# Scatter of an edge-attention layer as four rounded-type passes, with the edge rows split on GpSimd and new per-engine lists

## The reference

```python
e = jnp.einsum('behd,hd->beh', leaky_relu(Qs + Kt, 0.2), a) + jnp.log(A0[src, dst] + EPS)[None, :, None]
attn = ex / denom[src]                       # softmax over the edges of one source node
Y = jax.ops.segment_sum(attn[..., None] * Vt, src, num_segments=n)
return Y.reshape(bt, n, d) @ W_out.T
```

## Time and profile before

| what | value |
|---|---|
| median of 3 runs | 1133.86 us (1133.8 to 1134.31) |
| the profiled execution's own time | 1133.88 us |
| its span, first to last instruction | 1132.0 us |
| mean granted TensorE clock, share of full speed | 0.989 |
| instructions | 21408 |

### The profile page before, as it was taken

The page is one execution under the profiler, slowest core; times in us unless marked ns, Lnnn a source line. Parts: engine busy times, 40 slices in busy tenths (PEclk is TensorE's granted clock), DMA queues, the critical chain, the costliest instruction groups (busy, mean ns, idle before and its releaser), DMA issues. The chain is left out here.

```text
span 1132.0 us, 21408 instructions
## 1 busy us (share of the span) xinstructions
PE 1083.0 (96%) x7105; PEld 866.6 (77%) x7105; DVE 853.7 (75%) x3073; ACT 757.9 (67%) x1640; POOL 344.9 (30%) x465
## 2 busy tenths in 40 slices
...
DMA packets 132941, 89.42 MB, mean 79 GB/s; under 512 B 13664, under 2 KB 115424, under 8 KB 132832
## 3 DMA queue, kind: packets, MB, share of 16 engines
...
...
## 5 line engine op out<-in xcount | busy, mean ns | idle before, releaser
L2360 ACT ACTIVATE att_Es<-att_Ts,att_small 128x512 f32<-128x512 f32 x256 | 184.9, 724 | 8.9 <-DVE att_small L2457 8.2
L2457 DVE CUSTOM_DVE_ANT_0 att_Ts<-bank,mask_att 128x512 f32<-128x512 f32 x256 | 172.0, 683 | 22.4 <-PE bank L2612 18.3
L2369 ACT COPY att_PTs<-bank 128x512 f32<-128x512 f32 x248 | 144.5, 583 | 51.9 <-PE bank L2665 51.1
L2665 PE MATMUL bank<-ident,att_Es 128*128 128x128 f32 x1024 | 155.8, 275 | 6.8 <-ACT att_PTs L2369 6.6
L2665 PEld LDWEIGHTS bank<-ident,att_Es 128*128 128x128 f32 x1024 | 121.3, 142 | 42.8 <-ACT att_PTs L2369 17.3
L2612 PE MATMUL bank<-K_parts,Q_parts 128*128 128x512 f32 x256 | 113.1, 471 | 5.5 <-DVE att_small L2457 3.9
L2154 POOL TENSOR_SCALAR n_rs<-n_mv 128x4 f32<-128x4 f32 x46 | 15.5, 338 | 282.4 <-DVE n_mv L2149 282.4
L1597 PE MATMUL bank<-G_hi,UT_parts 128*128 128x384 f32 x288 | 79.1, 345 | 1.8 <-DVE G_lo L1440 1.8
L567 PE MATMUL bank<-gat_whs,gat_ETs 128*128 128x128 f32 x512 | 63.7, 280 | 2.0 <-PEq L149 2.0
L784 POOL TENSOR_SCALAR l_rs<-l_mv 128x4 f32<-128x4 f32 x16 | 3.8, 236 | 198.6 <-DVE l_mv L1064 198.2
L2612 PEld LDWEIGHTS bank<-K_parts,Q_parts 128*128 128x128 f32 x256 | 45.5, 190 | 24.2 <-issue 13.5
...
## 6 DMA issues: line engine op xcount, KB each, us to landing
Q_parts<-q_hi SPq DMA_DIRECT2D x128, 64.0 KB, 2.2
Q_parts<-q_lo SPq DMA_DIRECT2D x128, 64.0 KB, 2.0
K_parts<-k_hi SPq DMA_DIRECT2D x128, 64.0 KB, 2.0
K_parts<-k_lo SPq DMA_DIRECT2D x128, 64.0 KB, 2.0
...
```

The source lines that it names most:

```text
L2360: nc.scalar.activation(att_E[:, j % RING_E, :], att_T[:, j % RING_T, :], ACT.Exp, scale=-1.0, bias=att_small[:, 0, j:j + 1], accum_out=att ...
L2369: nc.scalar.copy(att_PT[:, h, :, cols(q)], c2[:].rearrange("p (s q) -> p s q", q=P)).then_inc(sem("att_pt"), 1)
L2457: nc.vector.tensor_tensor_reduce(att_T[:, j % RING_T, :], [c0, c1][j % 2][:], k.mask_att[:, tile_of(n, j)[1], :], -QK_SCALE, HUGE, ALU.add ...
L2665: mm = nc.tensor.transpose(dst[:, cols(s)], att_E[:, i % RING_E, cols(s)], k.ident[:])
```

## The change

edge_scatter now multiplies two parts of U, U_hi and U_lo, each in the type float32r, by src_rows, which is stored as float32r too: four matmuls where two stood. A new GpSimd step, edge_parts, makes the parts once edge_u is done: U_hi is a copy of U into float32r, U_lo is U - U_hi. edge_scatter waits for edge_parts (edge_ulo) instead of edge_u. The parts lie in the memory of edge_hgs, which is free between edge_v and edge_yT. The scratch gb gets a name of its own, fc_rows, at the same place as src_rows. In the front edge_parts(0) is the last GpSimd step. FILL_ORDER, ORDER and DRAIN_ORDER are new for all engines; every step and batch that was there is there again, and edge_parts is added to GpSimd's lists. The diff, without FILL_ORDER and DRAIN_ORDER:

```diff
--- before.py
+++ after.py
@@ -50,7 +50,7 @@
     edge_x edge_lcol edge_xz edge_le edge_exp edge_scattered edge_yT gat_done edge_stat edge_z edge_lb edge_max
     edge_lc edge_den edge_rden edge_attn edge_v edge_u x3_stored cheb_h edge_done ffn_y3 gat_turned gat_zloaded
     gat_loaded gat_aggr gat_vareps gat_rs gat_small gat_exp gat_s2 gat_hT gat_wh gat_pv gat_whs gat_max
-    gat_eturn gat_eT gat_stat gat_normed gat_T gat_rinv
+    edge_uhi edge_ulo gat_eturn gat_eT gat_stat gat_normed gat_T gat_rinv
 """.split()
 
 
@@ -103,7 +103,9 @@
         with ExitStack() as front:
             zsplit = sb("z_split", [P, 2, 2, N], R32, front)
         edge_pick = sb("edge_pick", [P, NT, 2 * E], R32)
-        src_rows = sb("src_rows", [P, ET, N])
+        with ExitStack() as front:
+            fc_rows = sb("fc_rows", [P, ET * N], F32, front)
+        src_rows = sb("src_rows", [P, ET, N], R32)
         seg_bias = sb("seg_bias", [P, ET, E])
         same_src = sb("same_src", [P, ET, E])
         logA = sb("logA", [P, ET])
@@ -133,7 +135,7 @@
                    x1_dram=x1_dram, x3_dram=x3_dram, res_dram=res_dram, v_dram=v_dram, rowv=rowv, b1c=b1c,
                    ident=ident, ones=ones, neg_half=neg_half, lap_hi=lap_hi, lap_lo=lap_lo, mask_gat=mask_gat,
                    mask_att=mask_att, zsplit=zsplit, edge_pick=edge_pick, src_rows=src_rows, seg_bias=seg_bias,
-                   same_src=same_src, logA=logA, W1ga=W1ga, head_a4=head_a4, G_hi=G_hi, G_lo=G_lo)
+                   same_src=same_src, logA=logA, fc_rows=fc_rows, W1ga=W1ga, head_a4=head_a4, G_hi=G_hi, G_lo=G_lo)
 
 
 
@@ -187,8 +189,11 @@
         def sb(name, shape, dt=F32):
             return c.enter_context(nc.sbuf_tensor(name, shape, dt))
 
-        e = Shared(h2=sb("edge_hs", [P, NT, D]), x3=sb("x3", [P, NT, D]), h2_hi=sb("h2_hi", [P, NT, D], R32),
-                   h2_lo=sb("h2_lo", [P, NT, D], R32), hg=sb("edge_hgs", [P, 2 * E]), xz=sb("edge_xzs", [P, E]),
+        with ExitStack() as in_hg:
+            U_hi, U_lo = (in_hg.enter_context(nc.sbuf_tensor(n, [P, E], R32)) for n in ["edge_uhi", "edge_ulo"])
+        hg = sb("edge_hgs", [P, 2 * E])
+        e = Shared(U_hi=U_hi, U_lo=U_lo, hg=hg, h2=sb("edge_hs", [P, NT, D]), x3=sb("x3", [P, NT, D]), h2_hi=sb("h2_hi", [P, NT, D], R32),
+                   h2_lo=sb("h2_lo", [P, NT, D], R32), xz=sb("edge_xzs", [P, E]),
                    junk=sb("edge_junk", [P, ET * H, E], BF16), small=sb("edge_small", [P, 6, ET * H]),
                    U=sb("edge_us", [P, ET * D]), stat=sb("edge_stat", [P, NT, 6]), mv=sb("edge_mv", [P, NT, 2]),
                    rs=sb("edge_rs", [P, 4, NT]))
@@ -200,6 +205,7 @@
     g = k.edge
     h2, x3, h2_hi, h2_lo, hg, xz, small, U = g.h2, g.x3, g.h2_hi, g.h2_lo, g.hg, g.xz, g.small, g.U
     zT, YT, x2, W = xz, hg, k.gat.x2, k.W
+    U_hi, U_lo = g.U_hi, g.U_lo
     b0, b1 = k.bank[4], k.bank[5]
 
     def cols(t):
@@ -237,7 +243,13 @@
             nc.gpsimd.tensor_tensor(h2_lo[:], h2[:], h2_hi[:].bitcast(F32), ALU.subtract
                                     ).then_inc(sem("edge_hlo"), 1)
 
-        return {"edge_rstd": edge_rstd, "edge_lo": edge_lo}
+        def edge_parts(n):
+            ready_alone(pool, "edge_u", n)
+            nc.gpsimd.tensor_copy(U_hi[:], U[:]).then_inc(sem("edge_uhi"), 1)
+            ready(pool, "edge_uhi", n)
+            nc.gpsimd.tensor_tensor(U_lo[:], U[:], U_hi[:].bitcast(F32), ALU.subtract).then_inc(sem("edge_ulo"), 1)
+
+        return {"edge_rstd": edge_rstd, "edge_lo": edge_lo, "edge_parts": edge_parts}
 
     def on_scalar(act):
         def edge_apply(n):
@@ -376,10 +388,11 @@
             mm.then_inc(sem("edge_den"), 1)
 
         def edge_scatter(n):
-            ready(pe, "edge_u", n)
+            ready(pe, "edge_ulo", n)
             for e in range(ET):
-                mm = nc.tensor.matmul(b0[:], U[:, cols(e)], k.src_rows[:, e, :], start=(e == 0),
-                                      stop=(e == ET - 1))
+                for i, part in enumerate([U_hi, U_lo]):
+                    mm = nc.tensor.matmul(b0[:], part[:, cols(e)], k.src_rows[:, e, :],
+                                          start=(e == 0 and i == 0), stop=(e == ET - 1 and i == 1))
             mm.then_inc(sem("edge_scattered"), 1)
 
         def edge_out(n):
@@ -622,7 +635,7 @@
         S = [k.lap_hi, k.lap_lo]
         sqr = k.mask_att[:].rearrange("p t m -> p (t m)")
 
-        gb = [k.src_rows[:].rearrange("p e n -> p (e n)")[:, i * D:(i + 1) * D] for i in range(STEPS)]
+        gb = [k.fc_rows[:, i * D:(i + 1) * D] for i in range(STEPS)]
         gb.append(k.seg_bias[:, 0, 0:D])
         node_col = sb("node_col", [P, NT])
         edge_ci = sb("edge_ci", [P, 2, ET], I32)
@@ -859,6 +872,7 @@
             edge["edge_rstd"](0)
             edge["edge_lo"](0)
             gat["gat_rstd"](1)
+            edge["edge_parts"](0)
 
         @block.scalar
         def _(act):
@@ -1830,6 +1844,7 @@
         gat_exp2 gat_exp3 gat_eT0 gat_eT1 gat_eT2 gat_eT3 gat_rstd load_z load_x
     """.split(),
     "edge": """
+        edge_parts
         edge_lc
         edge_gather0 edge_gather1 edge_x edge_lb0 edge_lb1 edge_lcol edge_v edge_den edge_scatter edge_out
         edge_stats edge_aggr edge_z edge_max0 edge_max1 edge_max2 edge_max3 edge_le edge_rden edge_attn edge_u
@@ -1861,205 +1876,208 @@
 
 ORDER = {
     "PE": """
-        att_turn12+ att_score14+ att_score15+ edge_out+ att_turn13+ gat_pv1+ att_turn14+ att_score0 att_score1 cheb_v+
-        att_turn15+ att_rows+ att_pv0+ att_pv1+ att_score2 gat_turn att_turn0 att_score3 ffn_wo+ cheb_prop0 cheb_prop1
-        att_score4 gat_wh cheb_g att_turn1 att_score5 ffn_turn+ att_turn2 att_score6 gat_s2 ffn_up0+ ffn_up1+
-        att_turn3 att_score7 att_score8 ffn_down0+ att_turn4 ffn_down1+ cheb_x1turn att_turn5 edge_gather0
-        edge_gather1 att_score9 att_turn6 att_score10 edge_x cheb_q att_turn7 edge_lcol att_score11 gat_eturn0
-        att_turn8 edge_lb0 gat_eturn1 att_score12 edge_lb1 att_score13 cheb_k gat_eturn2 gat_eturn3 att_turn9 edge_v
-        edge_den att_turn10 gat_pv0 att_turn11 edge_scatter
+        edge_v+ att_score14+ att_turn10+ edge_den+ gat_pv0+ att_turn11+ att_score15+ gat_pv1+ att_turn12+
+        edge_scatter+ att_score0 att_turn13+ att_score1 edge_out+ att_turn14+ cheb_v+ att_turn15+ att_rows+ att_pv0+
+        att_pv1+ att_turn0 att_score2 gat_turn att_score3 ffn_wo+ att_turn1 cheb_prop0 cheb_prop1 att_score4 gat_wh
+        att_score5 cheb_g att_score6 ffn_turn+ att_turn2 gat_s2 ffn_up0+ att_turn3 att_score7 ffn_up1+ att_score8
+        att_turn4 ffn_down0+ att_score9 ffn_down1+ att_turn5 cheb_x1turn edge_gather0 att_turn6 edge_gather1 cheb_q
+        edge_x att_turn7 att_score10 gat_eturn0 att_score11 edge_lcol att_turn8 att_score12 edge_lb0 gat_eturn1
+        edge_lb1 att_score13 cheb_k att_turn9 gat_eturn2 gat_eturn3
     """.split(),
     "DVE": """
-        edge_u+ n3_aggr++ gat_rinv+ cheb_klow+ n3_apply++ gat_stats att_mask14+ att_mask15+ edge_x3+ cheb_stats
-        cheb_aggr att_rv+ gat_aggr gat_x2a+ att_mask0 gat_x2b+ edge_stats att_mask1 gat_apply edge_aggr cheb_lo
-        att_scale+ att_mask2 att_mask3 ffn_y2+ n2_stats+ n2_aggr+ att_mask4 n2_apply+ cheb_y att_mask5 n1_stats
-        att_mask6 n1_aggr gat_scores0 n1_apply att_mask7 gat_scores1 cheb_x1 ffn_y3+ gat_scores2 gat_scores3 att_mask8
-        gat_row1 gat_row2 gat_max0 gat_row3 att_mask9 gat_max1 att_mask10 edge_z gat_max2 gat_max3 edge_lc att_mask11
-        cheb_qlow edge_max0 edge_max1 edge_max2 edge_max3 edge_le att_mask12 att_mask13 n3_stats+ edge_rden edge_attn
+        att_mask12+ edge_le+ n3_stats++ att_mask13+ cheb_klow+ n3_aggr++ edge_rden+ att_mask14+ edge_attn+ edge_u+
+        n3_apply++ att_mask15+ att_rv+ gat_stats att_mask0 gat_aggr gat_rinv+ att_mask1 edge_x3+ cheb_stats gat_x2a+
+        cheb_aggr gat_x2b+ gat_apply edge_stats edge_aggr att_scale+ att_mask2 cheb_lo ffn_y2+ n2_stats+ att_mask3
+        n2_aggr+ att_mask4 n2_apply+ att_mask5 cheb_y att_mask6 n1_stats gat_scores0 n1_aggr att_mask7 n1_apply
+        gat_scores1 cheb_x1 ffn_y3+ gat_scores2 att_mask8 gat_scores3 gat_row1 gat_max0 gat_row2 gat_max1 gat_row3
+        att_mask9 gat_max2 edge_z att_mask10 att_mask11 edge_lc gat_max3 cheb_qlow edge_max0 edge_max1 edge_max2
+        edge_max3
     """.split(),
     "ACT": """
-        att_copy12+ att_exp14+ att_exp15+ att_copy13+ att_copy14+ att_copy15+ cheb_apply att_exp0 cheb_hi cheb_vout+
-        att_spread+ att_exp1 att_copy0 att_exp2 gat_hT att_exp3 edge_apply cheb_xpT gat_wh_out0 att_exp4 edge_hi
-        att_copy1 gat_wh_out1 ffn_x2T+ att_copy2 ffn_gelu0+ ffn_gelu1+ att_copy3 att_exp5 att_copy4 att_exp6 att_exp7
-        att_copy5 cheb_x1T att_exp8 edge_hg gat_exp0 att_copy6 edge_xz gat_exp1 att_copy7 cheb_qsplit att_exp9
-        gat_exp2 gat_eT0 gat_exp3 att_copy8 gat_eT1 att_exp10 gat_eT2 edge_exp att_copy9 gat_eT3 cheb_ksplit att_exp11
-        att_copy10 att_exp12 att_exp13 att_copy11 edge_yT
```

(20 more changed lines are left out.)

274 lines of the change are left out of this document (135 added, 139 removed).

## The result

The change made the kernel slower: 1144.33 us median of 9 runs (1138.49 to 1146.44) against 1134.06 (1128.59 to 1137.69, 9 runs), a ratio of 1.0086 with a 95% interval of 1.0068 to 1.0104. The prediction was 1126.0, range 1116 to 1136. The profiled execution took 1144.34 us.

What follows compares the result with a forecast made beforehand. TensorE was taken to bound the middle. Batches 3 to 14 give -9.5 us, batch 2 -0.4, batches 1 and 15 +0.2, front +0.6, ties +1.2: together -7.9, to 1126.0 us, range 1116 to 1136.

Steps and rivals of the forecast that it cites:

- The bound: Middle batches: TensorE, busy 42.77 of 43.17 us, sets the pace, as long as VectorE, 2.4 us behind, follows.
- The passes: edge_scatter on TensorE: four rounded passes of 0.23 us instead of 1.72 us, saving 0.79 us a batch.
- The split: edge_parts on GpSimd: 1.8 us (1.1 to 2.0), its latency hidden in the middle and costed at nothing there.
- rival D: TensorE at edge_scatter: the scatter waits in every batch; 1142 us, range 1136.2 to 1146; chance 0.13.
- The lists: New order on all engines: a tie of 0 to 0.5 us on TensorE, charged 0.1 us a batch, 1.2 in all.
- rival C: VectorE at n3_apply: edge_parts on GpSimd blocks it up to 1.8 us, VectorE becomes the bound; 1132 to 1136; chance 0.13.
- gat_apply: VectorE: its first pass, held up beside ffn_final, is freed by the new order, 0.9 us a batch.
- I take nothing: Stretches outside the middle: no gain or loss from the new lists, with 3 us both ways kept for the range.

Runs made afterwards that it cites:

- f2: f1 with ffn_x3b and ffn_final also moved behind edge_rstd on GpSimd; 1133.14 us, 0.9982 of the kernel before.
- r1: f2's middle lists, with the old lists and the old plain f32 scatter outside the middle; 1129.91 us, 0.9953 of the kernel before.
- e3: The new scatter in the lists of the kernel before, edge_parts ahead of n3_rstd on GpSimd; 1139.02 us, 1.0040 of the kernel before.
- e2: The changed kernel's new lists with the old scatter and no edge_parts; 1139.37 us, 1.0047 of the kernel before.
- f1: e3 with n3_apply behind two masks, ffn_res ahead of n3_g, and some scatters and n3_apply later outside the middle; 1138.88 us, 1.0056 of the kernel before.
- g1: The changed kernel with n3_apply behind gat_apply on VectorE, n3_g behind cheb_rstd and ffn_x3b behind ffn_res on GpSimd; 1136.15 us, 1.0019 of the kernel before.
- e1: The changed kernel with n3_apply moved behind att_mask15, att_rv, gat_stats and att_mask0 in VectorE's middle list; 1139.47 us, 1.0049 of the kernel before.
- h1: The kernel before with ffn_final moved behind edge_rstd on GpSimd; 1135.18 us, 1.0014 of the kernel before.
- r2: r1 with cheb_x1 ahead of gat_scores1 in VectorE's middle list; 1128.15 us, 0.9939 of the kernel before.
- r3: The kernel before with cheb_x1 ahead of gat_scores1 in VectorE's middle list; 1132.68 us, 0.9987 of the kernel before.
- e4: The changed kernel with cheb_xpT of batch 0 ahead of edge_apply of batch 1 in ScalarE's beginning list; 1143.79 us, 1.0075 of the kernel before.
- r4: The changed kernel with the plain f32 scatter and no edge_parts in batches 0 to 4 and 15; 1144.35 us, 1.0080 of the kernel before.

## Why the prediction was wrong

**The bound** was read rightly: in f2 and r1 a saving on TensorE does come out of the batch, 0.56 and 0.50 us of it (the ten batches by ten). The condition that came with it, that VectorE follows, is what the change did not meet.

**The passes** were mis-sized by a little: 0.72 us saved, not 0.79. Passes two to four follow after 0.22 to 0.23 us as the earlier trace rows said; the first takes 0.32, as it comes behind a transpose. (Rows 5 print 0.40 where the prediction says 0.39, and 4 x 0.23 is 0.92; neither moves the sum.)

**The split** took 0.40 + 0.73 us and ended 1.21 us after it began, at the low end of the bounds; the cast, taken as 0.9, was the error. The hand-over of 0.1 us, for which no row was named, took 0.08 (743.37 to 743.45). That its latency is hidden in the middle was right: no scatter waits for edge_ulo there, and rival D did not happen; that the time lies in D's range, 1136.2 to 1146, is chance. Outside the middle the terms were on the careful side for the new lists, for which they were made: scatter 0 began 1.33 us after edge_u had ended, within the 1.2 to 2.0, batch 1 waited 0.3 us instead of 0.8, and batches 2, 3 and 15 not at all. In the old lists they would not hold: e3's waits of 0.7 to 1.2 us eat up what each scatter saves.

**The lists** are the step that failed: "in the new order I count a tie of 0 to 0.5 us, and charge 0.1 us a batch". Measured, a batch changed by -0.72 for the scatter, +0.30 of other busy time of TensorE and +1.06 of idle time (1.46 against 0.40): +0.64. The busy part is mostly e2's 0.22, of which scores that stand alone between transposes are a part; such a cost was not looked for. Busy time is not work alone, though: f1 and f2 have one list for TensorE, and 42.69 and 42.22 us of it. The idle part is the mechanism of rival C, held at 0.13. Its condition was left open and the profile after closes it: GpSimd comes first in every batch of the middle, since edge_u has ended by then and the CAST is the next instruction of its own queue behind n3_rstd, while VectorE waits for n3_rstd's signal and starts 0.07 us later. The Trainium skill, SBUF — State Buffer, section "SBUF: two separate sides", has this as an exclusive lock held for a whole instruction; the trace agrees with 0.40, 0.89 and 1.31 us for the three held passes of n3_apply, each ending 0.08 to 0.09 us after the GpSimd pass that held it. The trace does not agree for GpSimd's passes over 128x4, beside which n3_apply took 0.34 us as when alone; the measurement decides, and the last section has more of these.

C's price failed too. It counted two GpSimd passes, and a third, ffn_res, came from the list: 2.71 - 1.11 = 1.6 us of block is within its 1.8, but it set the cost by VectorE's sum of busy time and waits ("no gain", 1132 to 1136). VectorE is never full: 41.08 of 43.81 us. What the block costs is lateness in the chain mask, exp, transpose, copy, which TensorE meets 2 us behind the late mask (745.67 to 747.73), and which no sum of busy times shows. g1 takes away the block and the place of n3_apply together, 0.87 us a batch, with TensorE's list as it was; e1 takes the block alone and gets 0.27. So the two together are shown; their shares are not separable, since e1's place for n3_apply brought waits of its own, and no run leaves n3_apply where the change put it and takes GpSimd's passes away.

**gat_apply** was freed as forecast and is worth nothing by itself: h1. It counts only once n3_apply stands later and the steps behind it follow closely: f1 against f2, 0.75 us a batch, where the lateness of gat_rstd and the block went away together.

**Outside the middle** "I take nothing" was wrong by 1 to 4 us: 4.1 by the rest, 2.9 by the ends of the change, and 1.3 by those of e1, whose lists there are the same and whose granted clock from scatter 0 to 4 is that of the kernel before, 0.98. The rest of a single kernel is too coarse to lean on: it runs from +1.2 to +5.2 us with the new lists or edge_parts there and from -1.9 to +1.6 without both. The ends separate: 204.71 to 205.65 us with the old lists and the plain scatter there (before, h1, r1, r2, r3), 206.23 to 207.30 with the split in the old lists (e3, f1, f2), 206.04 to 208.81 with both the split and the new lists (the change, e1, e4, g1), 210.91 and 211.60 with the new lists and the plain scatter (e2, r4). So it is the new lists that cost there, 5.3 to 6.9 us with the plain scatter, and the split takes most of it back. A part of that can be the clock: it is 0.97 from scatter 0 to 4 in e2 and r4 and 0.98 before, and a front with 0.98 in place of 0.99 took 2.1 us longer (last section). The other 1.9 us of the change's trace, behind scatter 15, are no cost of the lists: h1, with the old steps there, took 94.92 us at a granted clock of 0.89, the change 93.68 at 0.91, the kernel before 91.78 at 0.96. Which step of the new lists costs time in the beginning stays open: e4 tried one and missed, and a middle list can't be joined to another beginning without writing that anew; this was not tried.
